# NVFP4 weights of an AdaLN block on one core: resident high and low parts, a four-step decoder, and the low parts shared out anew between GpSimd and VectorE

## The reference, cut to what matters

```
x = L0_attn_x                                   # (1, 1024, 256)
h = layernorm(x) * (1 + ca) + sa
x = x + ga * attention(h)                       # causal, latent 64, head 32
h = layernorm(x) * (1 + cb) + sb
Wg, Wu, Wd = dequant(gate), dequant(up), dequant(down)
#   dequant: two 4-bit codes per int32 word (low nibble first) -> table
#   [0,.5,1,1.5,2,3,4,6] with the sign in bit 3, times a scale per 32 values
inter = gelu_tanh(h @ Wg.T) * (h @ Wu.T)        # 1024 x 2048
x = x + gb * (inter @ Wd.T)
```

## Time and profile before

| | us |
|---|---|
| runs | 236.59, 239.24, 280.82 (median 239.24) |
| span of the profiled execution | 236.0 |
| PE busy | 200.2 (85%) |
| DVE busy | 162.0 (69%) |
| POOL busy | 105.7 (45%) |
| ACT busy | 84.9 (36%) |
| PE waits before its feed-forward products into gate and up | 18.9 |

### The profile page before, as it was taken

How to read it: one execution, slowest core, us unless ns; L and a number is a source line. 1 busy time by engine, 2 the same in 40 slices (tenths; PEclk the granted TensorE clock), 3 DMA queues, 4 the chain that set the end, 5 groups by cost and what they waited for, 6 DMA issues and landing times. The chain is left out here.

```text
span 236.0 us, 3087 instructions
## 1 busy us (share of the span) xinstructions
PE 200.2 (85%) x1064; PEld 159.2 (67%) x1064; DVE 162.0 (69%) x265; ACT 84.9 (36%) x143; POOL 105.7 (45%) x78
## 2 busy tenths in 40 slices
PE   7797896997679575977786969997989999999992
PEld 2483584754458355766675858886769888888991
DVE  1676978779799999999999991259583333333334
ACT  2100405151757231415160507743614535525230
POOL 4430418060517563665775928646235256236200
PEclk9979975699999999999999799999999999999997
DMA  6999765200000000000000000000020000000002
GB/s 193 342 288 212 201 202 178 99 3 0 0 0 1 0 3 0 1 0 0 1 3 0 0 0 3 0 0 0 0 92 0 3 0 0 0 0 0 3 0 89
DMA packets 5645, 11.31 MB, mean 48 GB/s; under 512 B 544, under 2 KB 2752, under 8 KB 5632
## 3 DMA queue, kind: packets, MB, share of 16 engines
q1 hardware_dynamic: 5216, 10.82, 15.5%
q10 hardware_dynamic: 416, 0.33, 0.6%
HBM read 10.09 MB, written 1.05 MB: 47 GB/s over the span
## 5 line engine op out<-in xcount | busy, mean ns | idle before, releaser
L853 PE MATMUL ps<-H,WS 128*128 128x512 f32 x384 | 97.2, 397 | 18.9 <-DVE wmod_sb L707 16.7
L853 PEld LDWEIGHTS ps<-H,WS 128*128 128x128 f32 x384 | 69.6, 189 | 36.9 <-DVE wmod_sb L707 21.0
L853 PEld LDWEIGHTS ps<-WS,IS 128*128 128x128 f32 x384 | 50.9, 194 | 4.2 <-issue 2.1
L853 PE MATMUL ps<-WS,IS 128*128 128x256 f32 x384 | 52.2, 287 | 1.5 <-DVE wmod_sb L707 1.3
L404 ACT ACTIVATE IS<-wmod_sb 128x512 fp32r<-128x512 f32 x32 | 20.2, 632 | 85.3 <-DVE wmod_sb L707 52.0
L495 POOL TENSOR_TENSOR WS<-wbuf,WS 128x1024 fp32r<-128x1024 f32 x16 | 40.4, 2526 | 8.9 <-ACT WS L385 8.9
L500 POOL TENSOR_TENSOR WS<-wbuf,WS 128x512 fp32r<-128x512 f32 x16 | 22.9, 1433 | 39.8 <-ACT WS L392 39.8
L707 DVE TENSOR_TENSOR wmod_sb<-ps,wmod_sb 128x512 f32<-128x512 f32 x32 | 22.0, 687 | 26.6 <-PE ps L853 22.2
L277 POOL TENSOR_TENSOR IS<-wmod_sb,IS 128x512 fp32r<-128x512 f32 x14 | 20.7, 1479 | 27.8 <-ACT IS L404 25.6
L277 DVE TENSOR_TENSOR IS<-wmod_sb,IS 128x512 fp32r<-128x512 f32 x18 | 12.8, 710 | 24.9 <-ACT IS L404 24.2
L398 ACT ACTIVATE wmod_sb<-ps 128x512 f32<-128x512 f32 x32 | 18.8, 586 | 6.4 <-PE ps L853 6.4
(11 more groups left out here) (117 smaller groups left out, 215.3 us busy)
## 6 DMA issues: line engine op xcount, KB each, us to landing
wbuf<-packed SPq DMA_DIRECT2D x8, 384.0 KB
wbuf<-scales SPq DMA_DIRECT2D x8, 384.0 KB
xres<-x SPq DMA_DIRECT2D x2, 512.0 KB, 6.2
wmod_sb<-wmod SPq DMA_DIRECT2D x1, 1024.0 KB, 10.5
out<-xres SPq DMA_DIRECT2D x4, 256.0 KB, 2.2
wmod_sb<-wmod SPq DMA_DIRECT2D x1, 512.0 KB, 6.6
rope_sb<-rope SPq DMA_DIRECT2D x1, 512.0 KB, 11.1
cst<-consts SPq DMA_DIRECT2D x1, 322.0 KB, 4.9
```

The source lines that it names most:

```text
L853: return pe.matmul(o, lhsT, rhs, start=start, stop=stop)
```

## The change

- `WH`, `WH6`, `WH7` (high parts) and `WL` (low parts) hold all 8 groups. `WL` lies on `W` (the old `wbuf`), so a low part overwrites the decoded values. To make room, `xn` has one half instead of two, `PF` lies under `PL`, and `rope_sb`, `chT`, `qk_h`, `prod` lie under the high parts of groups 6 and 7.
- ACT's `split_gu` and `split_d` become one `split_high(g)`, 1536 wide, once per group instead of twice. It waits for the group's decoding, and stands behind inter_hi(n) of odd n in the first half.
- POOL's low parts become `weights_low`, two instructions of 768 per group, once per group. POOL has no inter_low any more: DVE makes all 32, right behind inter_full(n) (and out_stack at n = 0).
- Decoding has 4 steps: two shift pairs on 768 words (s0, s1, which do not wait for each other), one mask over 1536 (s2), one multiply over 1536 (s3). EARLY is 3: groups 0, 1, 2 are decoded before inter_full(0), and groups 3 to 7 in units 0 to 9, two steps per unit.
- PE's second half is written out instead of looped, and waits for weights only in the first half.

```diff
-DECODE_STEPS = 7
-EARLY = 2
-POOL_UNITS = 2 * (GROUPS - 1)
-STEPS_AT_START = 8
+DECODE_STEPS = 4
+EARLY = 3
...
+        W = under("W", [P, GROUPS, 2, WORDS])
+        WL = sb("WL", [P, GROUPS, 2, WORDS], F32R)
...
+        def weights_low(engine, g, parts, done):
+            engine.wait_ge(w_hi, g + 1)
+            for e in parts:
+                engine.tensor_tensor(WL[:, g, e, :], W[:, g, e, :], high(g)[:, e, :].bitcast(F32),
+                                     ALU.subtract).then_inc(done, 1)
...
+            def split_high(g):
+                act.wait_ge(dec_done, g + 1)
+                if g >= GROUPS - 2:
+                    act.wait_ge(qk_ready, 4)
+                act.activation(high(g), W[:, g], ACT.Copy).then_inc(w_hi, 1)
...
             for n in range(UNITS + 2):
-                G = n // 2 + 1
-                if n % 2 == 0 and G > 1:
-                    split_gu(G, G % GROUPS)
                 gelu(n, n % 2, n >= 2)
                 if n == 0:
                     out_high(1)
                 inter_hi(n, n % 2, n >= 2)
-                if n % 2 and G > 1:
-                    split_d(G, G % GROUPS)
+                g = EARLY + n // 2
+                if n % 2 and g < GROUPS:
+                    split_high(g)
...
+            weights_low(pool, 0, range(2), w_lo_pool)
             rsqrt(N_LN2)
             for b in range(1, 2 * HT, 2):
                 probs_low(pool, 1, b, b + 1)
...
+            for g in range(1, EARLY + 1):
+                weights_low(pool, g, range(2), w_lo_pool)
+            rsqrt(N_LN2 + 1)
+            for g in range(EARLY + 1, GROUPS):
+                weights_low(pool, g, range(2), w_lo_pool)
...
+                        dve.tensor_scalar(dec[:, 0, :], bits, 28, 3, ALU.logical_shift_left,
+                                          ALU.arith_shift_right).then_inc(chain, 1)
...
+                        dve.tensor_scalar(dec[:, 1, :], bits, 24, 3, ALU.logical_shift_left,
+                                          ALU.arith_shift_right).then_inc(chain, 1)
...
+                        dve.tensor_scalar(dec[:], dec[:], -0x72000000, None, ALU.bitwise_and).then_inc(chain, 1)
...
+                        dve.scalar_tensor_tensor(W[:, g], vals, FP16_BIAS,
+                                                 W[:, g, 1, :].unsqueeze(1).to_broadcast([P, 2, WORDS]),
                                                  ALU.mult, ALU.mult).then_inc(dec_done, 1)
...
-                return STEPS_AT_START + 2 * n if n <= 3 else STEPS_AT_START + 6 + 7 * (n - 3) // 2
+                return min(DECODE_STEPS * n // 2, DECODE_STEPS * (GROUPS - EARLY))
...
             for n in range(UNITS + 2):
                 inter_full(n, n % 2, n >= 2)
                 if n == 0:
                     out_stack(1)
-                elif n >= POOL_UNITS:
-                    if n == POOL_UNITS:
-                        dve.wait_ge(i_lo, n)
-                    inter_low(dve, n, n % 2)
-
+                inter_low(dve, n, n % 2, n >= 2)
```

More of the change, by code:

```diff
@@ L72, in sb, with under @@
             return ctx.enter_context(nc.sbuf_tensor(name, shape, dt))
+        def under(name, shape, skip=0, dt=F32):
+            with nc.sbuf_tensor(name + "_skip", [P, max(skip, 4) // 4], F32) if skip else ExitStack():
+                with nc.sbuf_tensor(name, shape, dt) as t:
+                    return t
         def sem(name):
@@ L132, in build_block @@
         rden = sb("rden", [P, TILES])
-        PF = sb("PF", [P, RING, HALF])
         PH = sb("PH", [P, RING, HALF], F32R)
+        PF = under("PF", [P, RING, HALF])
         PL = sb("PL", [P, RING, HALF], F32R)
@@ L413, in _ @@
             v_high(1)
-            split_gu(0, 0)
-            split_d(0, 0)
+            split_high(0)
             qk_high(1)
@@ L690, in decode @@
                                                  ALU.mult, ALU.mult).then_inc(dec_done, 1)
             def decode_more(first, last):
-                for s in range(first, min(last, DECODE_STEPS * (GROUPS - EARLY))):
-                    decode(EARLY + s // DECODE_STEPS, s % DECODE_STEPS, s % DECODE_STEPS + 1)
+                for q in range(first, last):
+                    g, step = EARLY + q // DECODE_STEPS, q % DECODE_STEPS
+                    decode(g, step, step + 1)
             def steps_before(n):
-                return STEPS_AT_START + 2 * n if n <= 3 else STEPS_AT_START + 6 + 7 * (n - 3) // 2
+                return min(DECODE_STEPS * n // 2, DECODE_STEPS * (GROUPS - EARLY))
@@ L1089, in _ @@
                 if b == 2 * HT - 2:
-                    gate_up(0, 0, 0, 0, 0, first=True, later=False)
+                    gate_up(0, first=True, later=False)
                 if b >= 2:
@@ L1095, in _ @@
             pe.wait_ge(gb_out, 1)
-            gate_up(1, 0, 0, 0, 1, later=False)
+            gate_up(1, later=False)
             attend(1, b - 1, k - 1)
             attend(1, b, k)
-            for n in range(2, UNITS + 3):
-                gate_up(n, n // 2, n // UNITS, n // 2 % 2, n % 2, first=n == UNITS, after_own_banks=n == 2)
+            for n in range(2, 2 * UNITS):
+                gate_up(n, first=n == UNITS, after_own_banks=n == 2)
                 if n == 2:
@@ L1106, in _ @@
                     transpose2(1)
-                d = n - 2
-                down(d, d // 2, d // UNITS, d // 2 % 2, d % 2, first=d % UNITS == 0, last=d == UNITS - 1)
-            with pe.Fori(0, 3) as it:
-                for j in range(4):
-                    u, d = 3 + j, 1 + j
-                    gate_up(4 * it + (UNITS + u), 2 * it + (GROUPS + u // 2), 1, u // 2 % 2, u % 2)
-                    down(4 * it + (UNITS + d), 2 * it + (GROUPS + d // 2), 1, d // 2 % 2, d % 2)
-            n = 2 * UNITS - 1
-            gate_up(n, n // 2, 1, n // 2 % 2, 1)
-            for d in (n - 2, n - 1, n):
-                down(d, d // 2, 1, d // 2 % 2, d % 2, last=d == n)
+                down(n - 2)
+            for d in (2 * UNITS - 2, 2 * UNITS - 1):
+                down(d)
 def kernel(**inputs):
```

146 lines of the change are left out of this document (47 added, 99 removed).

## The result

| | before | changed |
|---|---|---|
| runs, us | 236.59, 237.94, 239.24, 280.82 | 244.06, 245.94, 246.07, 249.77 |
| median, us | 238.59 | 246.0 |
| span of the profiled execution | 236.0 | 244.3 |

The ratio is 1.031 with an interval of 1.023 to 1.039: slower by 3%. 241.5 had been forecast, in a range of 235 to 248.

What follows compares the result with a forecast made beforehand. It took DVE plus its exclusion with POOL to bound the first half, PE the second. 236.0 + 0.9 + 5.6 - 2.2 = 240.3, 240.9 with the time around the span, +0.6 for the clock: 241.5 us, range 235 to 248.

Steps and rivals of the forecast that it cites:

- ACT's queue: First-half units: split_high waits for decoding and holds up gelu; a pair takes 11.5 us against 10.9, five pairs +5.6.
- The prices: New instructions' durations, estimated from the earlier profile: s0, s1 0.56 us each, s2 0.96, s3 1.76, split_high 1.47, weights_low 1.86.
- Rival B: Decoding steps are dearer: +1.6 us per pair, 249.5 us in all, or 245.5 for half of it; chance 0.17.
- The exclusion: First half: DVE and POOL instructions on SBUF take turns whole; POOL's 3.7 us and DVE's 1.5 lie end to end.
- rival A: Exclusion between DVE and POOL hardly bites in the first half: a pair 9.9 us, total 233.5; chance 0.15.
- PE is no limit: First-half pair: PE's gate product for n+2 starts at 6.8 us, its up product ends near 9.9, before inter_full(n+2) at 11.5.
- Rival C: First half: ACT's wait is covered, only sums of DVE's and POOL's work count; pair 8.9 us, total 228; chance 0.07.
- The start: Up to inter_full(1): group 2's split ahead of gelu(0), inter_full(0) at 79.5 us, inter_full(1) at 85.0 against 84.08, +0.9.
- the clock: Falls of PE's clock, mostly covered in the first half by more than 1.5 us of slack per pair: +0.6 us.
- leftovers: Attention's residual1, stats2 and norm2 work in DVE's first-half units: 2.4 + 2.1 + 1.4 us over the five pairs.
- -2.2: Second half, bound by PE: without POOL's work, PE's waits of 1.24 and 0.98 us behind DVE go.
- what lies around the span: Time outside the profiled span: the fastest run shown lies 0.6 us above it, taking 240.3 to 240.9.

Runs made afterwards that it cites:

- split_later: Changed kernel with ACT's split_high for groups 3 to 7 one unit later, behind inter_hi of the following even unit; 231.99 us, ratio 0.973 to the kernel before.
- split_later_lead: split_later with group 2's split moved too, from ahead of gelu(0) and its table load to behind inter_hi(0); 233.27 us, ratio 0.979.
- warm_gaps: Changed kernel with unread products on zeros filling PE's waits before gate_up(5), (7), (9) and (11); 241.28 us, ratio 1.009.
- pe_unrolled: Kernel before with PE's second-half loop written out and nothing else; 239.01 us, ratio 1.001.
- no_pool_lows: Changed kernel without POOL's low parts of groups 3 to 7, PE reading those of groups 0 to 2 instead (output not the reference's); 243.76 us, ratio 1.025.

## Why the forecast came out as it did

The main steps, each against the changed kernel's trace:

- **ACT's queue: right, and shown.** A pair of 11.44 against 11.5, gelu's start 6.2 us behind inter_full(7) and the next inter_full at 6.9 are as worked out. split_later moves this one instruction, and the kernel gets 5.7% faster than the changed one (231.99 over 246.0).
- **The prices: right.** s0 and s1 0.55 (0.56 forecast), s2 0.95 (0.96), s3 1.76, split_high 1.48 (1.47), a low part of weights 1.82 (1.86). Rival B is out.
- **The exclusion: it bites, but is worth less than its length.** inter_low in even units takes 2.25, so rival A's pair of 9.9 didn't come. But the forecast's pair put POOL's 3.7 wholly on the path. Taken away, with the clock held, it gives back 0.73 a pair: behind it stood a wait of inter_hi for PE that the working said didn't exist ("PE is no limit").
- **Rival C, only the sums count:** not in the changed kernel. Its numbers (8.9, 228) came where the split's wait and DVE's detour by inter_low were both gone: 8.7 to 9.2 in the three middle pairs, 228.75 us.
- **The start:** inter_full(0) at 80.65 (79.5 forecast), (1) at 85.85 (85.0). In the profiled execution everything from 59 us on lay 1.8 later than before, behind a low clock at 22.3 to 29.1 us that had not been there. Other profiles, with the same code up to this point, have inter_full(0) at 78.4, 78.7, 79.6 and 79.9. So this part moves by 2 us from one execution to the next. ACT's wait for group 2 is there (3.53 us before inter_full(0)); split_later_lead, with the wait gone and nothing gained, gives no sign that it costs anything.

**The step that was mis-sized is the clock.** The working gave the falls +0.6 us, since "in the first half PE has more than 1.5 us of slack per pair". Stretches between inter_full, in us:

| | before | forecast | changed | warm_gaps |
|---|---|---|---|---|
| (1), start | 84.08 | 85.0 | 85.85 | 83.87 |
| (1) to (11) | 56.84 | 62.4 | 64.04 | 61.91 |
| (11) to (17) | 25.90 | 24.7 | 26.16 | 25.00 |
| (17) to (31) | 60.28 | 59.3 | 59.40 | 59.44 |

With PE kept at 2.4 GHz in its waits the forecast holds within 0.5 us in each of the last three stretches. Without it the first half is 2.1 us longer and the turn 1.2. The first half pair by pair (the forecast's 11.5 with the leftovers that it added to each):

| | (1) to (3) | (3) to (5) | (5) to (7) | (7) to (9) | (9) to (11) |
|---|---|---|---|---|---|
| forecast | 13.9 | 13.6 | 11.5 | 11.5 | 11.9 |
| warm_gaps | 13.78 | 13.47 | 11.43 | 11.44 | 11.79 |
| changed | 13.78 | 14.30 | 12.48 | 11.44 | 12.04 |

The clock of the changed kernel was at half from 107.6 to 114.4 us, which is unit 4 and the start of unit 5. Its rows there, DVE and ACT:

```profile
113.93 0.69 DVE L684 TENSOR_TENSOR wmod_sb<-ps,wmod_sb 128x512 f32<-128x512 f32 x1 [0.89 <-PE ps L823]
115.70 0.63 ACT L408 ACTIVATE IS<-wmod_sb 128x512 fp32r<-128x512 f32 x1 [3.73 <-PE ps L823]
116.42 0.69 DVE L291 TENSOR_TENSOR IS<-wmod_sb,IS 128x512 fp32r<-128x512 f32 x1 [1.80 <-ACT IS L408]
```

inter_full(5) waits 0.89 us for PE, and behind it inter_hi(5) for PE's down products, so that inter_low(5) shows 1.80 where 0.75 is usual. These two make up the 0.83 and 1.05 us of the two pairs, though the second carries no leftovers at all. The pair of 11.44 did not grow, but no fall lies in it, so it says nothing about slack. A fall can be free: pe_unrolled has one at 84 to 91 us that the kernel before hasn't, and both take 10.7 us from inter_full(1) to (3). So the slack of 1.5 us and more was a mean over the pair; what a fall costs is set by the waits that are near in the unit in which it lies.

At unit 11 PE goes into the half that it bounds. These are the rows there, from the changed kernel's timeline, PE and DVE:

```profile
145.33 1.22 PE L823 MATMUL ps<-H,WH 128*128 128x512 f32 x2 [3.38 <-ACT wmod_sb L402]
...
149.89 0.69 DVE L684 TENSOR_TENSOR wmod_sb<-ps,wmod_sb 128x512 f32<-128x512 f32 x1 [0.21 <-PE ps L823]
152.08 0.69 DVE L291 TENSOR_TENSOR IS<-wmod_sb,IS 128x512 fp32r<-128x512 f32 x1 [1.50 <-ACT IS L408]
```

Two products take 1.22 us here and 0.74 at 133.25; inter_hi and inter_low of the next unit stand behind PE's products (1.50 instead of 0.75), and PE brings no lead into the turn. The -2.2 forecast for the second half was half right for that reason: of the -0.98 of the later step -0.88 came (59.40 against 60.28), the -1.24 of the first was lost.

The Trainium skill (TensorE: Matmul & The Clock Gate, Why this matters for your kernels) says that gaps of PE between bursts of products drop its clock. 2 to 3 us more by it was in the working and set aside because the earlier trace rows showed one fall. This case agrees with the skill: 2.1 + 1.2 us come back when the gaps are filled. The earlier trace rows could not speak against it, for two reasons. It was read at waits of 1.8 to 2.6 us, and the change made four of them 2.7 to 4.7. And it is of one execution: pe_unrolled, with the same code there, has two falls.

A smaller term: I set 0.6 us for what lies around the span, from the profiled span and the fastest run shown. Where both are of one execution it is 1.8 to 2.1 (244.3 and 246.07; 237.3 and 239.1 for pe_unrolled). The span of 236.0 belongs then to an execution of about 237.9, such as the 237.94 in the result, and not to the fastest. So the miss of 4.6 in the profiled execution (246.07) is 1.2 around the span, 0.9 at the start, and 2.7 of the clock (2.1 + 1.2, less the 0.6 forecast); the prices and waits of the other stretches were 0.1 too high together (-0.5, +0.3, +0.1). That these three cancel is luck, though of half a microsecond only.

What stays open: why a unit of the second half goes at 4.21 us in all kernels that keep the weights in place and at 4.18 in those that don't. It isn't PE's code (pe_unrolled keeps 4.18), and it is worth about 0.5 us in all. Open too: why the four-step decoder alone gains 9 us, where 5 to 6 had been expected. In its profile, 8.4 us shorter than that of before, 7.0 lie between inter_full(1) and (11) (49.85 against 56.84), 1.9 ahead of (1), and 0.5 are lost behind (11).

## What to carry to other kernels

Before an instruction is put behind another in an engine's queue, ask what it waits for and what stands behind it: here ACT had 70% of its time free, and one split that waited for DVE held up gelu, PE and the clock. Do the parts of a change one by one, since a decoder worth 4% was hidden under an order that cost 7%. And sum the clock for each wait of PE by what follows it: here a fall cost nothing (units 1 and 2 of pe_unrolled), about 1 us in a pair where DVE and ACT then waited for PE, and 1.2 us at the turn, where PE is the bound behind it. One profile does not say how often it falls.

## What the runs showed of the hardware

- PE's granted clock fell to half (1.2 GHz) in or behind its waits between bursts of products, though not with each. In the changed kernel the waits of 4.27 and 3.38 us, before 108.41 and 145.33, have a fall (107.6 to 114.4 and 145.1 to 148.6); the fall of 87.1 to 97.4 began behind waits of 2.32 and 2.06 and before that of 4.69; the waits of 2.01 and 2.72, before 121.83 and 133.25, have none. A wait of 2.22 in the kernel before (129.64) and one of 2.02 in no_pool_lows (117.72) were each followed by a fall, others of that length were not. With products on zeros in four of the waits the clock was 1.00 from 97 us on (warm_gaps), where without them it fell twice.
- DVE and POOL on SBUF take turns by whole instructions, and both pay: inter_low 2.25 to 2.40 instead of 0.69, POOL's low part 2.19 instead of 1.82 when DVE has two in a row. What it costs is set by what waits behind: 1.56 us of one inter_low were worth 0.73 a pair.
- Shifts on 768 words with two operations each take 0.55 us, a mask over 1536 takes 0.95, and the multiply with a stride-2 half-word input and a broadcast second input 1.76.
